# Attention scores in two fp32r passes over a split strip, with VectorE's turned heads reordered

## The reference

```
q = rms_norm(x, qn_scale) @ q_w.T + q_b
k = rms_norm(x, kn_scale) @ k_w.T + k_b
v = x @ v_w.T + v_b
q, k = apply_rotary(q), apply_rotary(k)         # x*cos + x_rot*sin, per head
s = sigmoid(q @ k.T / sqrt(16))                 # per head: 512 x 512
out = (s / (sum of s over the keys + eps)) @ v  # heads side by side
return out @ o_w.T + o_b
```

## Time and profile before

| | |
|---|---|
| median of three runs | 1644.28 us |
| profiled execution, its own time | 1642.25 us |
| its span (first to last instruction) | 1640.5 us |
| attention's prologue | 592.0 to 622.5 us |
| attention's loop, first to last sigmoid | 622.5 to 1093.7 us |
| the tail to the next stage | 1093.7 to 1127.5 us |
| sigmoids | 128 of 1.88 us, 240.6 us |

### The profile page before, as it was taken

The page is one execution under the profiler, slowest core; times in us unless marked ns, Lnnn a source line. Parts: engine busy times, 40 slices in busy tenths (PEclk is TensorE's granted clock), DMA queues, the critical chain, the costliest instruction groups (busy, mean ns, idle before and its releaser), DMA issues. The chain is left out here.

```text
span 1640.5 us, 28867 instructions
## 1 busy us (share of the span) xinstructions
PE 1488.7 (91%) x10278; PEld 1150.0 (70%) x10278; DVE 1104.4 (67%) x2330; ACT 899.3 (55%) x1120; POOL 414.4 (25%) x413
## 2 busy tenths in 40 slices
PE   5899999869999977899999999875999999999998
PEld 4788888747788863334444444234989999999987
DVE  5577776578788783465565565335557777787868
ACT  2566655445555534565555655552336777777752
POOL 1122222230010031222224324222312333333330
PEclk8899999989999988999999999996999999999999
DMA  7000000210000000400000000003227888898864
GB/s 270 1 1 0 0 0 0 78 41 1 0 0 0 0 27 0 157 1 1 11 18 18 21 18 20 19 18 120 95 76 216 231 235 230 235 233 235 232 165 154
DMA packets 65453, 130.48 MB, mean 80 GB/s; under 512 B 8249, under 2 KB 38754, under 8 KB 64866
## 3 DMA queue, kind: packets, MB, share of 16 engines
q1 hardware_dynamic: 51074, 110.37, 21.6%
q0 software_dynamic: 14304, 19.15, 5.6%
HBM read 97.50 MB, written 32.00 MB: 79 GB/s over the span
## 5 line engine op out<-in xcount | busy, mean ns | idle before, releaser
L1760 ACT ACTIVATE at_wide<-at_sc_ps 128x2048 f32<-128x2048 f32 x128 | 240.6, 1880 | 171.5 <-PE at_sc_ps L1608 171.5
L1608 PE MATMUL at_sc_ps<-at_qT,at_kT 32*128 32x512 f32 x1024 | 150.1, 656 | 40.5 <-ACT at_wide L1760 38.0
L2188 POOL DMA_INDIRECT sums<-e_y,e_row_ids x78 | 121.9, 1563 | 247.5 <-ACT e_y L2343 235.6
L52 PE MATMUL e_gate_ps<-e_h_parts,e_w 128*128 128x256 f32 (+1 forms) x1128 | 176.9, 304 | 6.6 <-DVE e_w L2397 3.1
L2397 DVE TENSOR_TENSOR e_w<-e_raw,e_w 128x1024 fp32r<-128x1024 f32 x123 | 147.1, 1223 | 42.8 <-ACT e_w L2296 42.8
L52 PE MATMUL e_up_ps<-e_h_parts,e_w 128*128 128x256 f32 (+1 forms) x1128 | 175.0, 302 | 0.0
L52 PEld LDWEIGHTS e_gate_ps<-e_h_parts,e_w 128*128 128x128 f32 x1128 | 155.3, 193 | 14.4 <-DVE e_w L2397 3.2
L52 PEld LDWEIGHTS e_up_ps<-e_h_parts,e_w 128*128 128x128 f32 x1128 | 155.1, 192 | 7.9
L1622 PE MATMUL at_o_ps<-at_wide,at_v_ones 128*32 128x512 f32 x1024 | 139.2, 616 | 1.3 <-ACT at_wide L1760 1.3
L2253 PE MATMUL e_down_ps<-e_w,e_hidden 128*128 128x256 f32 x936 | 127.9, 286 | 1.0 <-DVE e_hidden L2446 1.0
L2296 ACT ACTIVATE e_w<-e_raw 128x1024 fp32r<-128x1024 f32 x123 | 125.3, 1048 | 5.5 <-DMA e_raw<-in_experts 5.5
(11 more groups left out here) (349 smaller groups left out, 2610.0 us busy)
## 6 DMA issues: line engine op xcount, KB each, us to landing
e_raw<-in_experts SPq DMA_DIRECT2D x123, 512.0 KB, 4.6
...
```

Of the source, the lines that this page charges most:

```text
L52: last = pe.matmul(out, left(i), right(j), start=n == 0, stop=n == len(steps) - 1)
L1608: last = nc.tensor.matmul(sc_ps[:, m, :], kT[strip, par, quad % 2, quad // 2, k * P:(k + 1) * P], qT[strip, par, quad // 2, :], start=True ...
L1760: nc.scalar.activation(wide[:, u % 2, :], sc_ps[:].rearrange("p n s -> p (n s)"), ACT.Sigmoid, scale=float(HD) ** -0.5).then_inc(sig_done, 1)
L2188: pool.indirect_dma_start(c.sums_dram[:, :], bass.IndirectOffsetOnAxis(ap=row_ids[:, j % 2, t:t + 1], axis=0), y[:, j % 2, t, :], None, co ...
```

## The change

The scores are computed in fp32r instead of fp32. An fp32 number is split in a head (rounded to fp32r) and a rest. A strip of 32 partitions now holds one head instead of two: its 16 features stand in it twice. For the keys, the first 16 partitions hold the head and the other 16 the rest. For the queries, both hold the head in the first pass, and the second pass multiplies by the rest with signs set by `sign` and `odd`. Each unit then takes two passes of four strips.

- `add_turned` writes each head twice (128x1024 instead of 128x512), into a buffer of its own for even tiles and into the space of the batch's `hT` for odd ones. `at_v_next`, `at_gated_rows` and `at_rows` are gone too; that space serves for them, and `hT` is laid out by batch.
- `by_feature` turns 8 blocks of 128x128 for each tile instead of 4, 4 for the queries and 4 for the keys, each set in a bank of its own, and waits for the tile before to be kept.
- ScalarE keeps the heads (`heads_by_feature`, two ACTIVATEs of 128x512 for each tile, behind the sigmoids 9, 10, 13 and 14), VectorE then the rests (`keep_by_feature`, two SCALAR_TENSOR_TENSORs instead of three instructions; twice as many of half the size where b % 3 is 1).
- In TensorE's loop `queries_keys` for tiles 2 and 3 move from units 9 and 10 to 10 and 11, `by_feature` stands one tile in each of units 8, 9, 12 and 13, `next_by_feature` moves from 13 to 14, and the rank, the router's product and the first half of `make_rows` from unit 15 to unit 0 of the next batch.
- On VectorE both adds stand right behind their rotations, and `normalise` behind both; the logits and `place_tokens` move to the start of the next iteration.

The core of the difference:

```diff
-        qT, kT = sb("qT", [P, 2, KC, S]), sb("kT", [P, 2, 2, KC, S])
+        qT, kT = sb("qT", [P, 2, 6, S], F32R), sb("kT", [P, 6, S], F32R)
...
-                def by_feature(b, t):
-
+                def by_feature(b, t, which):
+
+                    kept = (qT_kept, kT_kept)[which]
                     pe.wait_ge(rot_done, NT * b + t + 1)
-                    for n in range(2 * KC):
-                        last = nc.tensor.transpose(bank(b, t)[:, n * P:(n + 1) * P],
-                                                   rotated[:, t % 2, n * P:(n + 1) * P], c.ident[:])
-                    last.then_inc(qkT_done, 1)
+                    if is_first(b):
+                        if which and t >= 2:
+                            pe.wait_ge(kept, t - 1)
+                    elif t % 2:
+                        pe.wait_ge(kept, NT * b + t)
+                    elif which:
+                        pe.wait_ge(qk_scaled, NT * b + t + 2)
+                    for quad in range(QUADS):
+                        at = (which * QUADS + quad) * P
+                        n = in_bank(b, quad)
+                        last = nc.tensor.transpose(strips_bank(b, t, which)[:, n * P:(n + 1) * P],
+                                                   twice(b, t)[:, at:at + P], c.ident[:])
+                    last.then_inc((qT_done, kT_done)[which], 1)
...
-                    for m in range(QUAD):
-                        strip = slice(MW * m, MW * (m + 1))
-                        last = nc.tensor.matmul(sc_ps[:, m, :], kT[strip, par, quad % 2, quad // 2, k * P:(k + 1) * P],
-                                                qT[strip, par, quad // 2, :], start=True, stop=True)
+                    pair = pair_of(b, quad)
+                    for part in (HEAD, REST):
+                        for m in range(QUAD):
+                            strip = slice(MW * m, MW * (m + 1))
+                            last = nc.tensor.matmul(sc_ps[:, m, :], kT[strip, 2 * pair + quad % 2, k * P:(k + 1) * P],
+                                                    qT[strip, part, 2 * pair + quad % 2, :], start=part == HEAD, stop=part == REST)
...
+                        if u == 0 and b >= 2:
+                            pe.wait_ge(next_done, b - 1)
+                            if b >= 3:
+                                ds.rank(pe, b - 3, ranks)
+                            route(b - 2)
+                            if b >= 3:
+                                ds.make_rows(pe, b - 3, 0, a_ps[:, 1, :])
...
+                def heads_by_feature(b, t):
+
+                    cols = slice(t * P, (t + 1) * P)
+                    act.wait_ge(qT_done, NT * b + t + 1)
+                    nc.scalar.activation(in_pairs(qT[:, HEAD])[:, pairs(b), :, cols], by_pairs(strips_bank(b, t, 0)), ACT.Identity,
+                                         scale=sign[:, 0:1]).then_inc(q_head_done, 1)
+                    act.wait_ge(kT_done, NT * b + t + 1)
+                    nc.scalar.activation(in_pairs(kT[:])[:, pairs(b), :, cols], by_pairs(strips_bank(b, t, 1)), ACT.Copy
+                                         ).then_inc(k_head_done, 1)
...
-                        if past and u == 14:
+                        if coming and u in (9, 10, 13, 14):
+                            heads_by_feature(b + 1, {9: 0, 10: 1, 13: 2, 14: 3}[u])
+                        if past and u == 15:
                             modulate(b - 1)
...
-                        if b >= 3 and u in (0, 1):
-                            ds.keep_rows(act, b - 3, u, a_ps[:, 1, :])
-                        if b >= 2 and u == 3:
+                        if b >= 3 and u in (1, 3):
+                            ds.keep_rows(act, b - 3, u // 2, a_ps[:, 1, :])
+                        if b >= 2 and u == 2:
...
-                    nc.vector.tensor_tensor(rotated[:, buf, :], rotated[:, buf, :], turned[:, buf, :],
+                    nc.vector.tensor_tensor(twice(b, t).rearrange("p (h u d) -> p h u d", u=2, d=HD), cosines, sines,
                                             ALU.add).then_inc(rot_done, 1)
...
                     if coming:
                         rotate(n, 2)
+                        add_turned(n, 2)
+                        rotate(n, 3)
+                        add_turned(n, 3)
                     if past:
                         normalise(p)
-                    if coming:
-                        rotate(n, 3)
-                        add_turned(n, 2)
-                        add_turned(n, 3)
                     keep_quad(b, 2)
                     if coming:
-                        keep_by_feature(n, 1 - par, 2)
-                        keep_by_feature(n, 1 - par, 3)
+                        keep_by_feature(n, 2)
+                        keep_by_feature(n, 3)
```

212 lines of the change are left out of this document (127 added, 85 removed).

## The result

Median of five runs: 1637.45 us after the change (1636.26 to 1638.98) against 1644.28 before (1644.13 to 1645.74). The ratio is 0.9957, with an interval of 0.9942 to 0.9971: faster, by 6.8 us. The forecast was 1618, with 1598 to 1637 as the range of the forecast and its two nearest rivals, and 1609 to 1629 as its own; the measured median lies 0.45 above the wider one. The profiled execution took 1638.98 us against 1642.25 before and 1616.3 worked out; the miss to be explained is therefore 22.7 us.

What follows compares the result with a forecast made beforehand. Scores and sigmoids taking turns on one set of banks, or TensorE in fuller units, bound the loop. 1642.25 - 35.5 (loop) + 5.5 (prologue) + 0.5 (tail) + 3.5 (clock) = 1616.3; median 2.0 above: 1618 us, range 1609 to 1629.

Steps and rivals of the forecast that it cites:

- the term for TensorE's clock: TensorE, units 13 to 15: more idle time ahead of the router's products brings three more 1.2 GHz stretches, adding 3.5 us.
- rival B: TensorE's loop clock falls much more often: two 1.5 us stretches in each of seven batches, 1635 us; chance 0.11.
- The two passes: TensorE's scores in each unit: two fp32r passes cost 0.53 us start to start; the scores-and-sigmoid cycle becomes 2.67.
- D: Score strips run one after the other in fp32r: scores cost 2.1 us, each unit 1.07 more, 1780 us; chance 0.03.
- ScalarE: Two head evictions a tile take 1.3 us, so units 8, 9, 12 and 13 can each stretch by 0.5.
- VectorE's adds and rests: VectorE's queue: an add of 1024 elements takes 1.22 us, perhaps 1.5 near GpSimd; a rest 0.75, 1.5 a tile.
- C: From tile 2's product to tile 3's rests, VectorE's chain sets the pace: 5 us later each, 1653 us; chance 0.08.
- Step 2: TensorE before unit 11's scores: tile 1's transposes wait for tile 0's rests, done at 7.2 us instead of 5.9.
- Steps 4 to 6: Second half: VectorE is done at 20.1 us, TensorE waits 2.1 before quad 2, then for tile 2's rests until 22.2.
- A: Second half of a batch: VectorE's queue is not late, so TensorE doesn't wait there; 1604 us, chance 0.18.
- Step 7: Batch end: sigmoid 15 ends at 24.9 us, then modulate 1.45 and sigmoid 0; scores of unit 1 at 28.3.
- Prologue: Ahead of the loop: adds, and rests behind the heads, start the first scores 5.5 us later than 620.35.

Runs made afterwards that it cites:

- e2_fill: Changed kernel with six unused 128x512 fp32r products added in TensorE's idle time between attend(15) and the scores of unit 1: 1619.35 us.
- e9_moments: Changed kernel with router's work back in unit 15, quad 2's copy and tile 2's rests earlier on VectorE, tile 0's rests ahead of the moments: 1602.77 us.
- e6_norest: Changed kernel with the second pass of the scores, the product with the queries' rest, left out: 1621.10 us.
- e3_dve: Changed kernel with VectorE's copy of quad 2 moved ahead of the rotation of tile 3 and the rests of tile 2 ahead of normalise: 1622.66 us.
- after_again: The changed kernel itself, unchanged, run once more on the chip of three other follow-up kernels: 1636.86 us.

## Why the prediction was wrong

The steps of the batch stood, but for one. The best test of them is e2_fill, the changed kernel without the low stretch at number 1, in batch 4, which has none at number 14 either:

```
                                       worked out   e2_fill, batch 4   after, batch 5
from unit 1 to unit 9                     28.4            28.9              32.0
from unit 9 to unit 1 of the next         28.3            28.3              29.5
```

**The step that failed: the term for TensorE's clock.** The prediction added "three such stretches: 3.5" and reasoned from units 13 to 15, the wait ahead of quad 2. It had put the router's products behind a ring unit at full speed and priced unit 0 at 5.95 without a thought for their clock, though the earlier trace rows showed the clock fall at just these products. Worked out from the runs, the low stretches cost: at number 1, 9.28, 9.25, 9.26, 9.27 against 6.11 to 6.15 with the filling, 12.6 for batches 3 to 6; 8.08 against 5.16 in batch 2, 2.9; 7.68 against 4.48 in batch 7, 3.2; at number 14, 1.0 us in three batches, 3.0. Together 21.7.

The sum starts from the measured loop of before, which holds three short low stretches of its own. They cost some 3.7: numbers 0 and 1 of batches 4 and 6 are 12.63 and 12.68 where batch 5 has 11.09, and numbers 2 and 3 of batch 7 are 0.6 above a ring unit. So the sum had room for 3.7 + 3.5 = 7.2 us of low clock, and 21.7 came: 14.5 of the 22.7 us.

This is rival B in its mechanism: low stretches in most batches at waits and weak products. That its time of 1635 comes so near is in part luck. It had fourteen stretches of 1.5 us; measured were six of 3.1 and three of 1.0. With the 3.7 of before they would come to 24.7, 3.0 too much, and that made up for a part of what the other terms lack. B had 0.11 because of the argument set against it, that the loop's clock is 0.98 although TensorE stands idle up to 1.06 us in every ring unit. That mean holds stretches in which strong work follows each short idle time. It says nothing of 1.7 us of idle time followed by 2.3 us of small products, and the changed order was the first to put these two together.

What remains of the 22.7 us is 8.2. In the loop it is 5.4: with the low stretches taken off, batch 0 lacks 1.5 of its gain, batch 2 1.1, batch 7 1.2, and the four full batches 0.4 each. Batch 0 runs its first 8.2 us at 1.2 GHz, 1.4 more than before, which is at most 0.7 of its 1.5; the rest was not traced further. Then 1.3 in the prologue, and 1.5 behind the loop, where kernels with the same code there differ by up to 5 us among themselves (545.5 us from the last sigmoid to the end in e9_moments, 550.7 in e2_fill), so no run ties this last part to the change.

Point by point:

- *The two passes.* 0.67 from scores to attend, above the bounds of 0.53 to 0.64. The prediction halved all of 1.07; only the part that a pass costs halves, 0.43 to 0.24, and 0.2 stays (e6_norest). The ring is 2.78, not 2.67. It shows in the ring units and in batch 0; elsewhere prices that were a little high made up for it (four transposes cost 0.41, from 930.03 to 930.44, and not 0.55), so it moved the sum little; that the two halves of a batch come out to 0.5 is in part this cancelling. The estimate by the Trainium skill ("TensorE: Matmul & The Clock Gate", Part 2, Back-to-back issue gap), 0.43 for two passes, was further off for this distance. For a pass by itself the trace agrees with the page better than with the row: 0.23 to 0.24 (e6_norest), where the page has 0.216 and the row of the prediction 0.267. What neither had is the fixed 0.2.
- *D, strips that don't overlap.* Out: eight matmuls in 0.74.
- *ScalarE.* The heads take 0.68 and 0.60 a tile, 1.28 (1.3 taken). Its idle time is 121.8 (about 130 expected).
- *VectorE's adds and rests, C.* 1.31 and 1.57, 0.74: the means are as taken. C named adds of more than 1.6 as its sign, and four single adds of 2.33 are there, but at tile 1, where nothing waits for them; the adds of tiles 2 and 3, which C's place needs, took 1.22 to 1.23. So C is out. The Trainium skill's rule on the shared port ("SBUF — State Buffer", SBUF: two separate sides) would let a single add wait for a whole GpSimd instruction. The trace agrees: in batches 1 to 6 the add of tile 1 starts while GpSimd's L1518 runs and ends 1.08 to 1.09 us behind its end (1.46 us long in batches 1 and 2, 2.33 in 3 to 6), where an add with nothing beside it takes 1.21 to 1.23. The prediction went by the mean, in which this does not show; the trace of before has it too, with a median of 0.68 for the adds of 512 elements and 0.98 to 1.16 for the eight in the first half of batches 3 to 6.
- *Step 2.* Right: number 10 is 4.28, and 3.09 with the wait taken away (e9_moments).
- *Steps 4 to 6, and A.* The wait ahead of quad 2 is 1.78 in batch 4 (2.1 worked out), 11.6 us in 7 times in the loop; A is out. Taking it away gives 14.8 us, clock included (e3_dve).
- *Step 7.* Number 15 is 3.47 with modulate in it and 2.78 follow: right (3.4 worked out for modulate, sigmoid and what lies between).
- *Prologue.* 6.8 against 5.5 in the profiled execution, 5.0 in that of after_again.
- *What would show it.* Of the signs for it, the third quad's wait and ScalarE's idle time came. The ring, the distance from scores to sigmoid (919.11 to 919.96, 0.85 instead of 0.73) and the first sigmoid (629.3 instead of 628) were off by 0.1 to 1.3. The pitch of about 6 did not shrink to 3.7: number 1 was 6.20 and is 9.26, and the 3.68 stand at number 2. That sign was named for the wrong unit, since the sum itself had 5.95 there. The sign against it, a clock below 0.95 in the loop (0.94), came, and it was the one that decided.

The order that follows from this was run: e9_moments leaves the fp32r passes, the adds and the heads as the change has them, takes the router's work back to unit 15 and moves three entries of VectorE's queue. It is 2.5% below the kernel before, where the change alone is 0.4% below.
